# Moving a context batch's normalisation into the steps of the next batch, in a one-core Perceiver block

## The reference

```
x = x + xattn(ctx, layernorm(x), mask)   # cross attention, 16 heads of 64
x = x + attn(layernorm(x))               # self attention, 16 heads of 8, ALiBi
x = x + ffn(layernorm(x))                # int8-like fake quantisation, SiLU gate

def xattn(x, latents, mask):
    xn = layernorm(x) ; ln = layernorm(latents)
    q = ln @ Wq ; k, v = split(concat(xn, ln) @ Wkv)
    out = softmax(where(mask, q k^T / 8, -max)) v      # mask opens only late keys
    return layernorm(out @ Wout)
```

## Time and profile before

| | |
|---|---|
| median of 3 executions | 900.16 us (897.63 to 900.94) |
| the profiled execution | 900.01 us, span 898.0 us, mean TensorE clock 0.963 |
| PE, PEld | busy 832.3 us (93%), 445.9 us (50%) |
| DVE | busy 594.8 us (66%) |
| ACT | busy 450.5 us (50%) |
| POOL | busy 186.5 us (21%) |

### The profile page before, as it was taken

How to read it: one execution, slowest core, us unless ns; L and a number is a source line. 1 busy time by engine, 2 the same in 40 slices (tenths; PEclk the granted TensorE clock), 3 DMA queues, 4 the chain that set the end, 5 groups by cost and what they waited for, 6 DMA issues and landing times.

```text
span 898.0 us, 20741 instructions
## 1 busy us (share of the span) xinstructions
PE 832.3 (93%) x6742; PEld 445.9 (50%) x6743; DVE 594.8 (66%) x1515; ACT 450.5 (50%) x757; POOL 186.5 (21%) x354
## 2 busy tenths in 40 slices
PE   5699999999999999999999999999999999999753
PEld 4344544545454555545454545545454645455522
DVE  5777666666657576766657566766666576747577
ACT  5365454546465545546464545545465554443242
POOL 3011021212122221212222221211222222212101
PEclk9799999999999999999999999999999999999655
DMA  6113221111212121111212111201212111110001
GB/s 204 34 41 103 80 56 40 37 55 52 58 40 54 51 55 54 46 29 52 58 40 55 50 55 55 55 20 52 58 41 59 49 53 53 40 41 17 4 1 47
DMA packets 98347, 45.82 MB, mean 51 GB/s; under 512 B 72100, under 2 KB 90376, under 8 KB 98184
## 3 DMA queue, kind: packets, MB, share of 16 engines
q1 hardware_dynamic: 98256, 45.34, 18.2%
q10 hardware_dynamic: 56, 0.05, 0.0%
HBM read 25.69 MB, written 3.26 MB: 32 GB/s over the span
## 4 chain that ended last, share of the span: by engine, by line
PE 71%; DVE 17%; issue 6%; ACT 3%; DMA 1%; DVEq 1%; POOL 1%; ACTq 0%; SPq 0%; POOLq 0%
PE bank L1299 20%; PE bank L1353 7%; PE bank L1272 6%; PE bank L1227 5%; PE bank L1274 4%; PE bank L1276 4%; DVE mx L1694 4%; PE bank L1244 4%; PE bank L1370 3%; PE bank L1414 3%; DVE xf_all L1723 3%; PE bank L1389 2%; PE bank L1399 2%; PE bank L1243 2%; ACT arena L971 1%
## 5 line engine op out<-in xcount | busy, mean ns | idle before, releaser
L986 ACT ACTIVATE p<-bank,maskbias 128x512 f32<-128x512 f32 x224 | 154.2, 688 | 232.6 <-PE bank L1276 231.1
L1299 PE MATMUL bank<-p,xv 128*128 128x512 f32 (+1 forms) x512 | 238.0, 616 | 0.3 <-POOL arena L840 0.3
L1694 DVE TENSOR_REDUCE mx<-bank 128x1 f32<-128x512 f32 x256 | 165.5, 682 | 53.2 <-PE bank L1244 52.8
L1690 DVE TENSOR_TENSOR qkl_l<-bank,qkl_h 128x512 f16<-128x512 f32 x64 | 41.1, 685 | 76.7 <-ACT qkl_h L974 76.7
L1299 PEld LDWEIGHTS bank<-p,xv 128*128 128x128 f32 (+1 forms) x512 | 74.9, 188 | 31.5 <-issue 23.8
L1272 PE MATMUL bank<-qkc_h,xtT_h 128*128 128x512 f16 (+1 forms) x256 | 86.9, 389 | 0.0
L1244 PE MATMUL bank<-xtT_h,qkc_h 128*128 128x448 f16 x256 | 86.7, 358 | 0.0
L1274 PE MATMUL bank<-qkc_l,xtT_h 128*128 128x512 f16 (+1 forms) x256 | 85.0, 379 | 0.0
L1276 PE MATMUL bank<-qkc_h,xtT_l 128*128 128x512 f16 (+1 forms) x256 | 85.0, 379 | 0.0
L1243 PEld LDWEIGHTS bank<-ltT,qkl_h 128*128 128x128 f16 x256 | 24.9, 97 | 95.4 <-DVE mx L1694 53.9
L1353 PE MATMUL bank<-arena,wvF 128*64 128x128 f32 x1024 | 69.3, 278 | 0.0
(11 more groups left out here) (260 smaller groups left out, 1461.1 us busy)
## 6 DMA issues: line engine op xcount, KB each, us to landing
arena<-den_dram SPq DMA_DIRECT2D x62, 128.0 KB, 3.2
qkc_h<-arena SPq DMA_DIRECT2D x30, 256.0 KB, 2.4
qkc_l<-arena SPq DMA_DIRECT2D x30, 256.0 KB, 2.4
raw<-in_ctx SPq DMA_DIRECT2D x32, 192.0 KB, 2.5
raw<-in_ctx SPq DMA_DIRECT2D x64, 32.0 KB, 2.2
lt<-lt_dram SPq DMA_DIRECT2D x60, 31.8 KB, 2.1
arena<-in_L_xattn_Wkv SPq DMA_DIRECT2D x1, 1024.0 KB, 6.7
ltT_dram<-x_all SPq DMA_DIRECT2D x4, 256.0 KB, 3.5
```

The lines of the kernel that those rows point to most:

```text
L986: a.activation(p32[0:r, slot, :], sbank[t % SRING][0:r, :], ACT.Exp, bias=bias).then_inc(s_probs_ready, 1)
L1299: op = mm(bk[:, :], rows_of[at, :], p32[at, slot, :], start=tile < 2, stop=tile in (0, plan.TILES - 1))
L1694: v.tensor_reduce(mx[:, hq_tile, part:part + 1], bk[:, 0:width], AX.X, ALU.max).then_inc(s_jobs_taken, 1)
```

## The change

In the plan of the branch in use, `STATS` and `AGGR` go from step 4 to 5, `RSTD` from 4 to 6, and `XHAT` and `MASK` from step 6 to "step 8", which is step 0 of the following batch: the loops now call `ahead` a second time per step, with the batch that is one nearer and t + 8. The transposes follow: job T of the odd batch goes from step 0 to 1, that of the even batch from 7.5 to 9. `MOVE` goes from step 8 to 11. Since `den_rows` waits for it, the `RDEN` of the odd half goes from its step 3 to 5, and `rden_rows` of the odd half goes behind `load_rows` in SP's queue. The two denominators are added by a tensor_reduce in place of a tensor_tensor. The other branch's plan keeps its steps.

```diff
 WINDOW = Plan(N - 448, dict(
-    STATS={4: (0, 4)}, AGGR=4, RSTD=4, XHAT=6, MASK=6,
+    STATS={5: (0, 4)}, AGGR=5, RSTD=6, XHAT=8, MASK=8,
-    ODD=dict(T=[0], MAX=[2.5, 3, 3, 3.5, 4, 4, 4.5, 5], MT=6),
+    ODD=dict(T=[1], MAX=[2.5, 3, 3, 3.5, 4, 4, 4.5, 5], MT=6),
-    EVEN=dict(T=[7.5], MAX=[10.5, 11, 11, 11.5, 12, 12, 12.5, 13], MT=14), XV={2: (0, 4)},
-    RDEN=3, MOVE=8, ...
+    EVEN=dict(T=[9], MAX=[10.5, 11, 11, 11.5, 12, 12, 12.5, 13], MT=14), XV={2: (0, 4)},
+    RDEN=(3, 5), MOVE=11, ...

@@ SP, end of each half of a turn
-                        if since or k == 1:
+                        if since and k == 0:
                             rden_rows(b - 1, 1 - par, pair)
-                        if since and k == 0:
                             load_x(i - 1)
+                        if more and k == 1:
+                            load_rows(plan, i, last, 1 - par)
+                        if k == 1:
+                            rden_rows(b - 1, 1 - par, pair)
...
-                        if more:
+                        if k == 0:
                             load_rows(plan, i, last, 1 - par)

@@ POOL and DVE, each step of a turn
+                            ahead(plan, i * 2 + k + 1, 1 - k, t + plan.STEPS)
                             prep(...)
                         if not last:
                             ahead(plan, i * 2 + k + 2, k, t)

@@ DVE, normalise
-                if t == plan.at["RDEN"]:
+                if t == plan.at["RDEN"][k]:
...
-                    v.tensor_tensor(rcol[:, :], dcol[:, 0, :], dcol[:, 1, :], ALU.add).then_inc(s_dsum_ready, 1)
+                    v.tensor_reduce(rcol[:, :], dcol[:, :, :].rearrange("p z c -> p c z"), AX.X, ALU.add).then_inc(s_dsum_ready, 1)
```

More of the change, by code:

```diff
@@ L154 @@
     EVEN=dict(T=[28.5, 29.5, 30.5, 31.5], MAX=[39 + m // 3 + 0.5 * (m % 3 > 0) for m in range(32)], MT=51), XV={8: (0, 3), 9: (3, 6), 10: (6, 9), 11: (9, 11), 12: (11, 13)},
-    RDEN=8,
+    RDEN=(8, 8),
     MOVE=28, ST1=[10, 11, 14, 15], YN=[13, 17], XB=18, ST2=19, M0=21, P0=21, X1=22, X1B=23, M1=22, P1=23, XH=24, XHT=25, XHT_OUT=26, QKV=27, QKV_OUT=28,
@@ L159 @@
 WINDOW = Plan(N - 448, dict(
-    STATS={4: (0, 4)}, AGGR=4, RSTD=4, XHAT=6, MASK=6,
+    STATS={5: (0, 4)}, AGGR=5, RSTD=6, XHAT=8, MASK=8,
     START=dict(QP=[-3, -3], QC=[-2, -2], QL=[-1, -1], T=[-2.5], MAX=[1, 1, 2, 2, 3, 3, 4, 4], MT=5),
-    ODD=dict(T=[0], MAX=[2.5, 3, 3, 3.5, 4, 4, 4.5, 5], MT=6),
+    ODD=dict(T=[1], MAX=[2.5, 3, 3, 3.5, 4, 4, 4.5, 5], MT=6),
     NEXT=dict(QP=[0, 0.5], QC=[1.5, 6.5], QL=[8.5, 9.5]),
-    EVEN=dict(T=[7.5], MAX=[10.5, 11, 11, 11.5, 12, 12, 12.5, 13], MT=14), XV={2: (0, 4)},
-    RDEN=3, MOVE=8, ST1=[3, 4, 5, 6], YN=[6, 7], XB=7, ST2=8, M0=9, P0=9, X1=10, X1B=15, M1=10, P1=10,
+    EVEN=dict(T=[9], MAX=[10.5, 11, 11, 11.5, 12, 12, 12.5, 13], MT=14), XV={2: (0, 4)},
+    RDEN=(3, 5), MOVE=11, ST1=[3, 4, 5, 6], YN=[6, 7], XB=7, ST2=8, M0=9, P0=9, X1=10, X1B=15, M1=10, P1=10,
     XH=12, XHT=13, XHT_OUT=13, QKV=14, QKV_OUT=14, VBLK=15, KEXP=15, SC=16, ALIBI=[17, 18], SMAX=22, SHIFT=22, EXP=23,
@@ L852, in attention @@
                 pool.wait_ge(s_mask_made, 1)
-                for t in range(plan.STEPS):
+                for t in range(2 * plan.STEPS):
                     ahead(plan, 0, 0, t)
@@ L1705, in ctx_count, with normalise @@
                 return (n - par) * 8 * plan.CTX_DMAS + 16 * plan.CTX_DMAS
-            def normalise(plan, b, t):
-                if t == plan.at["RDEN"]:
+            def normalise(plan, b, k, t):
+                if t == plan.at["RDEN"][k]:
                     dve.wait_ge(s_den_col, 32 * b + 32)
@@ L1811, in attention @@
                 setup(plan)
-                for t in range(plan.at["XHAT"], plan.STEPS):
+                for t in range(plan.at["XHAT"], 2 * plan.STEPS):
                     ahead(plan, 0, 0, t)
@@ L1825, in body @@
                         more = not (last and k == 1)
+                        if more:
+                            ahead(plan, b + 1, 1 - k, t + plan.STEPS)
                         prep(plan, i, last, s - 0.5)
@@ L1829, in body @@
                             ahead(plan, b + 2, k, t)
[L1830 to L1833, removed]
+                        if since or k == 1:
+                            normalise(plan, b - 1, k, t)
                         background(plan, i, since, s, tail)
```

## The result

The changed kernel takes 992.96 us (median of 4 runs, 991.93 to 993.39) where the kernel before takes 900.16: a ratio of 1.1035 [1.1011, 1.1058], 93 us slower. The prediction was 980 us, within 948 to 1006.

A forecast was written before the change was run, and what follows sets the result against it. PE, busy 93% of the span, was taken as the bound. 14 turns of 4.6 us waits (64.4) plus 1.0 for turn 0 on 900.0 give 965, and 15 of clock 980 us; with rivals 948 to 1006.

The forecast's parts named there:

- The gap ahead of QP: Before QP in 14 turns: lq's load, issued at M (end of mT's cast) + 4.9, idles PE 3.6 us.
- T: Job T at its later steps makes PE wait 0.8 us before QL and 0.8 before QC, each turn.
- The waits that go: PE's waits at the second QP job and at a MAX job go, 0.3 us each per turn.
- The clock: TensorE's clock falls in each turn's idle gap ahead of QP, costing 1.1 us a turn, 15 us in all.
- Turn 0 and the end: Turn 0 has the rest without the gap, +1.0 us; turn 15 makes no queries, 0.
- the clock stays up: Rival, 25%: lq's load is late but the loop's clock does not fall; 965 us, 950 to 978.
- the load is not late: Rival, 7%: rden_rows costs SP nothing there, so only T's stalls are left; +15, 915 us.
- Faster: Rival, 5%: DVE's relief wins, lq comes before PE is ready and T hides under the values; 891 us.

The follow-up runs named there:

- e1: The changed kernel with the odd half's rden_rows sent in the next turn, behind the load of lq and the context load; 922.19 us.
- e3: The kernel before with only job T moved to its later steps (odd 1, even 9); 923.10 us.
- e7: The changed kernel with MOVE at 8, RDEN at 3 and SP's queue as before, keeping the later statistics, normalisation and transposes; 915.10 us.
- e2: The changed kernel with 14 matmuls of 128x512, results overwritten, put in front of QP's wait for lq; 966.98 us.
- e4: The kernel before with only MOVE at 11, the odd half's RDEN at 5 and its rden_rows behind load_rows; 942.94 us.
- e9: Kernel before with MOVE at 11, odd RDEN at 5, rden_rows behind next turn's first loads, odd T behind second QP, odd XHAT/MASK one step later; 895.20 us.
- e10: e9 with turn 0's two store_block calls ahead of load_rows again, as in the kernel before; 889.62 us.

## Why the prediction was right, and by how much its terms were off

The sign and the mechanism held, and the time lay 13 us above the forecast, inside the range. Term by term:

- **The gap ahead of QP.** Forecast: load issued at M + 4.9, PE ready at M + 4.12, the cast 0.5 us late, a gap of 3.6. Measured in the turn shown: issued at M + 4.99; PE ready at 592.37 (0.33 behind the start of row 1284, as in the earlier trace rows's turn, where that row starts at 530.05), M + 3.62, which is 0.5 sooner against a cast that is 0.5 later; PE starts at M + 7.17; a gap of 3.55. e1 takes all but 0.45 of it away (71 us with its clock). The reason that I gave for a slower landing is not borne out: `lq` lands in 2.1 us (median) behind the two broadcasts, and landed in 2.0 without them, while `xpair` behind its own still takes 2.5. I had taken 2.3; with the load issued 0.09 us later than forecast, and QP 0.08 us behind its landing, the start comes out as forecast all the same.
- **T.** Forecast 0.8 twice. Measured 0.73 and 0.74 (1.79 and 1.80 less 1.06), 23.4 us in 30 waits; e3 and e7 have them without the gap. That T would come later once the gap no longer covers XHAT did not happen: it is 23.4 us in e1 and 23.5 in e7.
- **The waits that go.** The second QP job's 0.21 us and half of the MAX waits (9.2 us in 27, now 5.2 in 14) went. With the two terms above I forecast 4.6 us of waits a turn; e2, where the clock stays up, shows 4.46.
- **The clock.** This term was mis-sized: 1.1 us a turn forecast, 2.0 measured, as 56.50 less e2's 54.50. I had taken the middle between nothing and 4.5 / 2 = 2.2 and the upper bound was near the answer: the clock fell in every turn. It makes 12 us over turns 2 to 14, 2 of which the smaller waits give back. That half of the slow working time is lost held: the 5.2 us of slow work from 595.92 to about 601.1 would cost 2.6 us and the 3.0 us from 540.08 would cost 1.5, and the turns of 56.9 and 55.8 us are 2.4 and 1.4 longer than e2's 54.4 over turns 3 to 14. The Trainium skill (TensorE: Matmul & The Clock Gate, "HAM oscillation — how this bites in real kernels") also reckons half of the throttled time as lost; the trace agrees, with these numbers.
- **Turn 1.** Missing from the sum: I costed `rden_rows` behind `load_rows`, and did not see that in turn 0 `load_rows` overtakes the two stores as well, so that these too stand in front of turn 1's load. Turn 1 grew by 9.2 us in place of 5.7.
- **Turn 0 and the end.** Forecast +1.0 and 0; measured +1.2 and -2.4. What makes the last turn and the end shorter was not tried, and that it takes back two thirds of what turn 1 has too much is chance.

These give 9.9 + 3.5 + 0.2 - 2.4 = 11.2 us more than the sum, which is the difference of the spans (92.0 less 80.8, from 64.4 + 1.0 + 15.4).

The rivals: "the clock stays up" fell with e2, "the load is not late" with e4 and e1, which is near the 915 us that I gave for it (922, with 0.38 us left in front of each QP). "Faster" needed both new waits to be hidden; neither was. What the relief of the MAX jobs is worth once nothing waits for `lq`, T or `kexp` is shown by e9: 50.04 to 49.64 us a turn.

**The parts do not add up.** The context steps alone cost 15 us (e7), the move of sums and its transfers alone 43 (e4), both together 93. The rest is where they meet: statistics and `RDEN` together delay the cast by half a microsecond (PE is ready for the first job at M + 3.62; with the statistics alone, in e7, it is M + 4.02, with `RDEN` alone, in e4, M + 4.12 as before), and T's transposes no longer cover half a microsecond ahead of QP. The idle time there goes from 2.4 to 3.5 us, and the clock falls in every turn in place of half of them, on average for longer.

## What to carry to other kernels

Where an in-order queue serves a load that the same turn needs, cost every instruction that a changed order puts in front of it, the written-out turns' one-off stores included: 2.8 us of store, wait and broadcast, with a cast half a microsecond later, became 3.6 us of idle TensorE and 2.0 more of lower clock. Find the transfer with the earliest need after a step, and send the late ones behind it; here that alone gave back 71 of 93 us. With that order, the late `MOVE` and `RDEN`, T where it hides and `XHAT` of the odd batch one step later, e10 is 1.1% faster than the kernel before. It does not have the move that the change is named for: with the normalisation in the next batch's steps, T has to come late and waits twice a turn (e7, 15 us). A few matmuls that do nothing useful, in front of a wait that can't be removed, are a cheap way to see how much of a loss is the clock's.

## What the runs showed of the hardware that was not expected

**The clock after about 2.4 us idle is not settled by the idle time.** In e4 it stayed at 2.4 GHz after 2.39 us and fell after 2.29 us in the next turn; over the loop, waits of 2.27 to 2.45 us left it up in 6 turns, and waits of 2.29 to 2.87 us were followed by a fall in 7. In these 7 turns it fell only when PE was at work again, after 9 to 12 more matmuls at full speed, and the same is seen in turn 1 of e9 (2.40 us idle). After 3.5 us, in the change, it fell in every turn. The cost of a fall was 1.6 us in e4 and 2.0 on average in the change.

**A copy on DVE is held until POOL's instruction beside it ends.** In the changed kernel:

```profile
591.28 1.50 DVE L1807 COPY x_all<-x 128x128 f32 x1
592.71 0.33 DVE L1727 TENSOR_SCALAR xf_all<-x,smv,srs 128x128 f32 x1
```

```profile
590.80 1.90 POOL L843 TENSOR_TENSOR arena<-kT,halfmask 128x1024 f32<-128x1024 f32 x1
```

The copy, 0.23 us (median) in the kernel before, ends at 592.78, and POOL's tensor_tensor at 592.70. Before, it is the tensor_scalar into `xf_all` that stands beside `kexp` and takes 1.93 us where it now takes 0.33. The Trainium skill (SBUF — State Buffer, "SBUF: two separate sides") says that GpSimd and certain instructions of VectorE take turns at one pair of ports, and the later one is held until the other's instruction ends; the trace agrees, with 1.50 against 0.23 us. In the changed kernel DVE is 61% busy and PE's waits lie elsewhere. In the kernel before the held tensor_scalar is 3% of the chain that ended last, ahead of the 0.21 us that the second QP job waits. No run here tries either kernel without it, so its cost is not shown.
